# Grouped layer of a transformer kernel: the first group's tiles stay in the ring, four PSUM banks for the early projections, the swap behind seven spills instead of eight, TensorE two units ahead in the dense part

## The reference

```python
router_scores = jax.nn.softmax(xt @ Wr + br, axis=-1)
fs = _grouped_routing_scores(router_scores)   # sort the tokens of each expert, sum the scores by 64,
                                              # keep the best groups, normalise over experts
up = jnp.einsum('td,edh->teh', xt, Wup) + bup
gate = jnp.einsum('td,edh->teh', xt, Wgate) + bgate
h = jax.nn.silu(up) * gate * fs[:, :, None]
out = jnp.einsum('teh,ehd->td', h, Wdown) + fs @ bdown
```

## Time and profile before

| | us |
|---|---|
| median of 3 runs | 2532.41 (2529.04 to 2540.9) |
| profiled execution | 2545.23 |
| its span | 2543.4 |
| early projections, sort beside them | 1415 to 1602 |
| rest of the routing | 1602 to 1713 |
| dense block | 1713 to 1983 |

### The profile page before, as it was taken

How to read it: one execution, slowest core, us unless ns; L and a number is a source line. 1 busy time by engine, 2 the same in 40 slices (tenths; PEclk the granted TensorE clock), 3 DMA queues, 4 the chain that set the end, 5 groups by cost and what they waited for, 6 DMA issues and landing times. The chain is left out here.

```text
span 2543.4 us, 47961 instructions
## 1 busy us (share of the span) xinstructions
PE 1852.9 (73%) x14115; PEld 1294.2 (51%) x14149; DVE 1643.0 (65%) x3886; ACT 835.4 (33%) x1896; POOL 808.9 (32%) x1153
## 2 busy tenths in 40 slices
PE   3999984212389987985997799217888799428883
PEld 2888872101256664653776233115666577415552
DVE  5888864689857653445676899575555477773332
ACT  1555541234444422322453577100000245202221
POOL 1555530135333233024331000002333133008884
PEclk9999995555589978996898899658999699555555
DMA  4444420000000041111003466405554000304445
GB/s 121 110 107 108 106 57 0 24 0 0 6 1 0 0 153 36 43 36 27 1 0 59 171 273 275 190 8 163 209 206 149 6 1 0 106 20 74 78 78 134
DMA packets 185139, 199.23 MB, mean 78 GB/s; under 512 B 102562, under 2 KB 164834, under 8 KB 176482
## 3 DMA queue, kind: packets, MB, share of 16 engines
q1 hardware_dynamic: 161570, 136.25, 17.6%
q10 hardware_dynamic: 9152, 47.29, 5.2%
q0 software_dynamic: 14336, 14.69, 3.4%
HBM read 106.33 MB, written 71.40 MB: 70 GB/s over the span
## 5 line engine op out<-in xcount | busy, mean ns | idle before, releaser
L2082 POOL TENSOR_TENSOR gr_tp<-gr_ring 128x512 f32<-128x512 f32 x64 | 81.9, 1280 | 491.4 <-POOLq L1835 316.6
L773 POOL TENSOR_TENSOR at_KM<-at_K,at_mask 128x512 f32<-128x512 f32 x96 | 100.0, 1041 | 309.7 <-ACT at_Q L860 309.7
L873 ACT ACTIVATE at_ET<-at_psT 128x512 f32<-128x512 f32 x192 | 114.6, 597 | 172.9 <-PE at_psT L824 172.6
L2150 PEld LDWEIGHTS gr_psY<-gr_wd,gr_h 128*128 128x128 f32 x1024 | 131.0, 193 | 69.1 <-DVE gr_h L2110 47.4
L2150 PE MATMUL gr_psY<-gr_wd,gr_h 128*128 128x128 f32 x1024 | 143.4, 283 | 25.8 <-DVE gr_h L2110 25.8
L910 DVE TENSOR_REDUCE at_mx<-at_psS 128x16 f32<-128x1024 f32 x96 | 117.6, 1225 | 61.6 <-PE at_psS L803 61.6
L249 ACT ACT_TABLE_LOAD x6 | 7.7, 1283 | 415.3 <-PEq L63 399.6
L803 PE MATMUL at_psS<-at_KM,at_Q 32*64 32x256 f32 x1536 | 135.3, 423 | 4.7 <-POOL at_KM L773 3.9
L437 POOL TENSOR_TENSOR at_E<-at_Z,at_mx 128x512 f32<-128x512 f32 x128 | 130.9, 1045 | 9.0 <-DVE at_mx L623 8.1
L824 PE MATMUL at_psT<-kept_ident,at_Z 128*128 128x128 f32 x768 | 131.6, 296 | 1.2 <-DVE at_Z L923 0.4
L2010 PE MATMUL gr_psE<-kept_xT,gr_wu 128*128 (+1 forms) x256 | 130.9, 621 | 1.6 <-ACT gr_ring L1877 1.5
(11 more groups left out here) (566 smaller groups left out, 4841.7 us busy)
## 6 DMA issues: line engine op xcount, KB each, us to landing
gr_spill<-gr_ring SPq DMA_DIRECT2D x32, 1536.0 KB, 5.1
gr_ring<-gr_spill ACTq DMA_DIRECT2D x28, 1536.0 KB, 6.5
at_amask<-mask_Bx16xSxS_ff SPq DMA_DIRECT2D x128, 128.0 KB, 2.8
at_amask<-at_amask SPq DMA_DIRECT2D x64, 256.0 KB, 3.3
gr_ring<-gr_spill SPq DMA_DIRECT2D x4, 1536.0 KB, 16.1
cap_acc<-cap_zero SPq DMA_DIRECT2D x2, 2112.0 KB, 12.5
cap_sums<-cap_acc SPq DMA_DIRECT2D x8, 512.0 KB, 7.5
ex_xs<-ex_zero SPq DMA_DIRECT2D x1, 2496.0 KB, 11.2
```

The lines of the kernel that those rows point to most:

```text
L773: pool.tensor_tensor(KM[:, s, :, :], K[:, s, :].unsqueeze(1).broadcast_to([P, 4, P]), mask4[:, :].unsqueeze(2).broadcast_to([P, 4, P]), AL ...
L873: act.activation(ET[:, 4 * a:4 * a + 4, :].rearrange("p r q -> p (r q)"), psT[:, a, :], ACT.Exp, scale=QK_SCALE).then_inc(exped, 1)
L2150: last = pe.matmul(psY[:, j, :], h[:, s % 2, j * P:j * P + P], wd[:, s, :], start=False, stop=(s == C - 1), skip_group_check=True)
```

## The change

1. SyncE's loop spills 7 groups, not 8. The projections take the groups in the order 1, 2, ..., 7, 0: `turn` counts, `g` is the group. Group 0 is last and stays in the ring; the four reads at L1851 go, and in the dense block the waits on `back` are for 16·g in place of 16·(g+1).
2. `gr_psE` goes, and the early projections use the four banks of `gr_psV`. For that TensorE waits for `v_taken` before them, and for all tiles to be taken before it uses `gr_psV` again.
3. In the dense block `gr_psF` has four banks and `gr_tg` two buffers, TensorE runs `(2, up), (0, down)`, and VectorE's `product` is split: `gate` (`gr_fst` and `gr_tg`) runs one unit ahead of `product` (`gr_h`), and stands in front of it in each step.

```diff
...
             m.part = "gr"
...
-            psE = pb("psE", [P, 2, 512], on=routing)
...
-                    def spill_group(g):
+                    with sp.Fori(1, GROUPS2) as g:
                         for u in range(CHUNKS):
-                            sp.wait_ge(taken, CHUNKS * TILES * g + TILES * (u + 1))
+                            sp.wait_ge(taken, CHUNKS * TILES * (g - 1) + TILES * (u + 1))
                             sp.dma_start(spilled_to(CHUNKS * g + u), slot_of(u)).then_inc(spilled[u], 16)
-
-                    spill_group(0)
-                    with sp.Fori(1, GROUPS2) as g:
-                        spill_group(g)
                     sp.wait_ge(swapped, 1)
...
                     for u in range(CHUNKS):
-                        sp.wait_ge(spilled[u], 16 * GROUPS2)
-                        sp.dma_start(slot_of(u), spilled_to(u)).then_inc(back[u], 16)
+                        sp.wait_ge(spilled[u], 16 * (GROUPS2 - 1))
...
                     act.activation(V[:, :], psV[:, :, :].rearrange("p a b -> p (a b)"), ACT.Copy).then_inc(v_taken, 1)
...
-                    def take_group(g):
+                    def take_group(turn):
                         for j in range(CHUNKS * TILES):
                             u, (k, is_up) = j // TILES, kind_of[j % TILES]
                             c = 4 * u + k
-                            act.wait_ge(multiplied, CHUNKS * TILES * g + j + 1)
+                            act.wait_ge(multiplied, CHUNKS * TILES * turn + j + 1)
                             if j % TILES == 0:
-                                wait_past(act, spilled[u], 16 * g)
+                                wait_past(act, spilled[u], 16 * turn)
                             bias = bu[:, c:c + 1] if is_up else bg[:, c:c + 1]
-                            act.activation(ring[:, u, j % TILES, :], psE[:, j % 2, :], ACT.Silu if is_up else ACT.Identity, bias=bias).then_inc(taken, 1)
+                            act.activation(ring[:, u, j % TILES, :], psV[:, j % 4, :], ACT.Silu if is_up else ACT.Identity, bias=bias).then_inc(taken, 1)
                     take_group(0)
-                    with act.Fori(1, GROUPS2) as g:
-                        take_group(g)
+                    with act.Fori(1, GROUPS2) as turn:
+                        take_group(turn)
...
-                    def multiply_group(g):
+                    pe.wait_ge(v_taken, 1)
+
+                    def multiply_group(turn, g):
                         x = m.xT[:, bass.ds(512 * g, 512)]
                         for j in range(CHUNKS * TILES):
                             u, (k, is_up) = j // TILES, kind_of[j % TILES]
                             c = 4 * u + k
                             w = (wu if is_up else wg)[:, EC * c:EC * c + EC, :].rearrange("p e h -> p (e h)")
-                            wait_past(pe, taken, CHUNKS * TILES * g + j - 1)
-                            pe.matmul(psE[:, j % 2, :], w, x, start=True, stop=True).then_inc(multiplied, 1)
-
-                    multiply_group(0)
-                    with pe.Fori(1, GROUPS2) as g:
-                        multiply_group(g)
+                            wait_past(pe, taken, CHUNKS * TILES * turn + j - 3)
+                            pe.matmul(psV[:, j % 4, :], w, x, start=True, stop=True).then_inc(multiplied, 1)
+
+                    multiply_group(0, 1)
+                    with pe.Fori(1, GROUPS2 - 1) as turn:
+                        multiply_group(turn, turn + 1)
+                    multiply_group(GROUPS2 - 1, 0)
...
                     pe.wait_ge(kept, 1)
+                    pe.wait_ge(taken, CHUNKS * TILES * GROUPS2)
                     for b in range(4):
                         last = pe.matmul(psV[:, b, :], mats[:, SAME_HALF, :], V[:, 512 * b:512 * b + 512], start=True, stop=True)
...
-            tp, tg, h = sb("tp", [P, 2, 512], on=second), sb("tg", [P, 512], on=second), sb("h", [P, 2, 512], on=second)
-            psG, psF = (pb(n, [P, 2, 512], on=second) for n in ("psG", "psF"))
+            tp, tg, h = sb("tp", [P, 2, 512], on=second), sb("tg", [P, 2, 512], on=second), sb("h", [P, 2, 512], on=second)
+            psG, psF = pb("psG", [P, 2, 512], on=second), pb("psF", [P, 4, 512], on=second)
...
                         first = GATED[s // 2 % 2]
-                        pool.wait_ge(back[s // 4], 16 * (g + 1))
+                        wait_past(pool, back[s // 4], 16 * g)
                         wait_past(pool, h_ready, q - 3)
                         pool.tensor_tensor(tp[:, s // 2 % 2, :], ring[:, s // 4, first, :], ring[:, s // 4, first + 1, :], ALU.mult).then_inc(pooled, 1)
...
-                    def product(q, s, g):
+                    def gate(q, s, g):
                         if s == 0:
                             wait_past(dve, down_done, q - C + 1)
                             dve.tensor_scalar(fst[:, :], fs[:, bass.ds(512 * g, 512)], 1.0, None, ALU.mult).then_inc(staged, 1)
+                        if s % 2:
+                            dve.wait_ge(up_ready, q + 1)
+                            wait_past(dve, back[s // 4], 16 * g)
+                            wait_past(dve, h_ready, q - 3)
+                            dve.scalar_tensor_tensor(tg[:, s // 2 % 2, :], psG[:, s // 2 % 2, :], bg[:, s:s + 1], ring[:, s // 4, WAITING[s // 2 % 2], :],
+                                                     ALU.add, ALU.mult).then_inc(gated, 1)
+
+                    def product(q, s, g):
                         dve.wait_ge(up_ready, q + 1)
-                        if s % 2:
-                            dve.wait_ge(back[s // 4], 16 * (g + 1))
-                            dve.scalar_tensor_tensor(tg[:, :], psG[:, s // 2 % 2, :], bg[:, s:s + 1], ring[:, s // 4, WAITING[s // 2 % 2], :],
-                                                     ALU.add, ALU.mult).then_inc(gated, 1)
-                            dve.wait_ge(gated, pairs(s, g))
-                        else:
-                            dve.wait_ge(pooled, pairs(s, g))
+                        dve.wait_ge(gated if s % 2 else pooled, pairs(s, g))
                         wait_past(dve, down_done, q - 1)
-                        product_of = tg[:, :] if s % 2 else tp[:, s // 2 % 2, :]
-                        dve.tensor_tensor(h[:, s % 2, :], psF[:, s % 2, :], product_of, ALU.mult).then_inc(h_ready, 1)
+                        product_of = tg if s % 2 else tp
+                        dve.tensor_tensor(h[:, s % 2, :], psF[:, s % 4, :], product_of[:, s // 2 % 2, :], ALU.mult).then_inc(h_ready, 1)
...
-                    run(dve, [(0, product), (-1, residual), (-2, measure)])
+                    run(dve, [(1, gate), (0, product), (-1, residual), (-2, measure)])
...
                     def up(q, s, g):
-                        wait_past(pe, h_ready, q - 1)
+                        wait_past(pe, h_ready, q - 3)
                         x = m.xT[:, bass.ds(512 * g, 512)]
...
                             pe.matmul(psG[:, s // 2 % 2, :], wg[:, EC * s:EC * s + EC, :].rearrange("p e h -> p (e h)"), x, start=True, stop=True)
...
                             pe.wait_ge(parts_in, 16 * 12)
                         k, e = divmod(EC * s, SOME)
-                        pe.matmul(psF[:, s % 2, :], pick[:, e:e + EC, :].rearrange("p e h -> p (e h)"),
+                        pe.matmul(psF[:, s % 4, :], pick[:, e:e + EC, :].rearrange("p e h -> p (e h)"),
                                   parts[:, k, bass.ds(512 * g, 512)], start=True, stop=True).then_inc(up_ready, 1)
...
-                    run(pe, [(0, up), (-1, down)])
+                    run(pe, [(2, up), (0, down)])
...
```

## The result

The changed kernel took 2514.78 us in the median of 5 runs (2512.89 to 2520.76), the kernel before 2536.14 beside it: a ratio of 0.9925, 95% interval 0.9901 to 0.9948, so by the ratio 19 us less, between 13 and 25; the two medians are 21 us apart. A second series gave 0.9921 (0.9894 to 0.9948). The forecast was 2512.2 in a range of 2500 to 2525.

What follows compares the result with a forecast made beforehand. Bounds: VectorE's 26.9 us wait at the swap in the routing block, and a loop through TensorE and VectorE in the dense block. Swap -20.7, banks 0, dense block +0.5: -20.2 from 2532.41 gives 2512.2 us, own range 2506 to 2524.

Steps and rivals of the forecast that it cites:

- The swap's wait: Routing block: VectorE's wait at the swap after the first sort falls from 26.9 to 6.2 us, gaining 20.7.
- Rival C: Routing block: spills still queue in front of the swap, its wait shrinks by only 9, 2524 us; chance 0.06.
- Four banks at nothing: Early projections: four banks may end them some 15 us earlier, but nothing waits for that: 0 on the path.
- The pair: Dense block: two units take 3.70 us, 0.11 less, in a loop through TensorE and VectorE.
- Rival A: Dense block runs at TensorE's pace, 3.18 us a pair, 30 us less for the block, 2482 us; chance 0.13.
- The group's end: Dense block: the pair at a group's end takes 5.4 us, making a group 31.3 us, 0.3 more than before.
- The dense block's sum: Whole dense block: gains and losses of pairs, group ends, start and end come out at +0.5 us.
- The start: Start of the dense block: one `down` fewer at TensorE's lower clock between the first two T, -1.8 us.
- Rival D: Dense block: TensorE loses its clock through 1.2 us pauses at group ends, all work doubles, 2646 us; chance 0.03.
- the bounds: Dense block: +7 us if `gr_h` starts 0.78 behind `gr_tg`, -3 if the group's end costs no more than before.
- Rival B: Dense block eats part of the gain: `gr_h` 0.78 behind `gr_tg`, dearer group ends, +9.5, 2521 us; chance 0.12.
- T: Dense block: start of the `down` that follows `gr_psG` and `gr_psF`; `gr_tg` was to start 0.20 us later.

Runs made afterwards that it cites:

- swap_only: Kernel before with only group 0 last and kept in the ring, seven spills, then the swap; two banks and dense block unchanged: ratio 0.9910, 2496.45 us.
- banks_only: Kernel before with only the early projections moved to the four banks of `gr_psV`, eight spills kept: ratio 0.9921, 2503.14 us.
- product_first: Changed kernel with VectorE's stages in the order product, residual, gate, so `gr_h` stands before the next unit's `gr_tg`: ratio 0.9780, 2464.73 us.
- tg_with_own_h: Changed kernel with `gr_tg` put back in front of its own unit's `gr_h`, only `gr_fst` one unit ahead: ratio 0.9768.

## Why the prediction was right, point by point

- **The swap's wait.** Forecast 6.2 us, measured 6.9; gain 20.7 against 20.0. Its halves landed in a median of 5.4 us, the 5.5 taken from `gr_fs<-gr_V`. The missing 0.7 us comes from using this median for the second half, which alone counts: it took 6.3 us, the first 4.4. By the Trainium skill (DMA: Bandwidth & Descriptors, Anatomy of one DMA) I had an estimate of about 5 us of wait. The section is about DMAs that GpSimd issues, and this one is SyncE's; the measured 6.9 decides, and the row of the trace was nearer. That the seventh spill needs the four banks is excluded by swap_only. Rival C, spills that pile up behind faster projections, is excluded by the changed kernel's own profile: the swap was issued 0.03 us behind the sort's end. The 9 us by which C let the wait shrink had no working behind them.
- **Four banks at nothing.** Shown by the pair swap_only and banks_only. The prediction did not say that the banks alone would have given 15 to 25 us; it follows from its own reading, that the swap stood behind the last spill.
- **The pair.** Forecast 3.70, measured 3.68, with each link as computed. That `gr_tg` in front of `gr_h` is the cause is shown by product_first and tg_with_own_h. Rival A was TensorE's pace; it needed one exchange, and TensorE's own pair is 3.08, not the 3.18 that I read from a pair of before. The first `down` of that pair, with 1.16 us in place of 1.05, took as long as one behind a wait.
- **The group's end.** Forecast 5.4, measured 5.42 where the clock stayed full. The interval of 3.87 in front of five of the seven ends was not forecast, though the kernel before has one of 3.90 at the same place. A middle group without a dip takes 31.36 us, forecast 31.3: this 0.19 and the 0.02 by which each pair was taken too long nearly cancel, which is luck.
- **The dense block's sum.** Forecast +0.5; 257.9, 254.2 and 254.1 us in three profiles of the new order against 254.6. The spread between the three comes from the clock: two dips (3.0 us) and a late rise at the start (first interval 5.8 us against 3.9 to 4.0) in the first of them, one dip in each of the others. The start was forecast 1.8 us shorter; the first interval, 7.69 before, became 1.9 shorter in the first profile and 3.7 to 3.8 in the others.
- **Rival D** was wrong in size and right in kind. I gave it 3 in 100 as a loss of the clock for the whole block. What happens is a dip behind some group ends, 1.1 to 1.7 us each, 1.1 to 3.0 us in each of the three profiles with the pause of 1.2. The term was missing from the sum; it is covered by the bounds. I had read the Trainium skill (TensorE: Matmul & The Clock Gate, What's actually happening) as saying that such a pause in a busy stretch does not count as idle; that reading of mine does not hold in these runs.
- Rival B is excluded for the pairs: `gr_tg` still started 0.20 behind T and `gr_h` 0.67 behind `gr_tg`, not 0.78. Only in front of the five middle ends did `gr_tg` start 0.40 behind T, 1.0 us in all.

The forecast's sum was 2.6 us below the measured time, less than the interval of the measurement. So small a difference is in part luck: the kernel before, with 2536.14 beside the changed one, was itself 3.7 above the 2532.41 that the sum starts from. What can be compared is the difference, 20.2 us forecast against 19 by the ratio, between 13 and 25. The terms, with +0.5 for the block, give a range of 2507 to 2523; the prediction's 2506 to 2524 is 1 us too wide at either end.

What stays open: why the way from the swap to the dense block was 1.6 us longer in the changed kernel's profile; it was 116.7 us against 115.1. In the eleven other profiles it lies between 115.3 and 116.6, with and without the change, so I take it for the spread between executions, without having shown it. Open too is why a dip follows one middle group end and not the next, and what makes the interval of 3.87.

## What to carry to other kernels

A lead on one engine is worth nothing if the partner's written order puts an operation of the leading unit in front of the one that is waited for: follow the loop through both lists before writing buffers for it. When two edits remove the same wait, test each alone; their gains do not add, and here either one would have done. Count a pause of the matrix engine at its length and also at what the clock may lose behind it.

## What the runs showed of the hardware

- In this dense block a pause of TensorE of 1.21 us was followed by the lower clock in 4 of 15 cases, one of 1.80 us in 8 of 10; pauses of 0.65 to 0.81 us in none of 14, and of 1.02 and 1.61 us, at the first and last group end only, in none of 10. Pauses of 0.33 to 0.46 us in the pairs were followed by none in any profile. Each time the clock came back by itself, and a dip cost 1.1 to 1.7 us.
- Two DMAs of 512 KB between partitions of the on-chip memory, with nothing beside them, were there 6.9 us after the request, the first 4.4 and the second 6.3 us after its own issue; with a spill and reads of 1.5 MB beside them 9.4 to 9.9.
- An independent VectorE operation starts 0.08 us before the end of the one in front, a dependent one 0.03 behind it. In a loop through two engines this was 0.11 of the 0.13 us by which a pair became shorter.
- GpSimd's `gr_tp` ran beside `gr_h` in the pairs of the changed kernel and beside `gr_h` and `kept_X` at its seven group ends, and took 1.27 us, as it did in 48 cases of the kernel before with nothing on VectorE beside it; `gr_h` and `kept_X` took 0.68 us, before 0.68 and 0.69. Beside `gr_fst`, which VectorE copies within the on-chip memory, `gr_tp` took 1.37 to 1.38 us, in 7 of 7 cases.
